# A six-stage perceiver block on one core: the first product of the closing feed-forward moved beside the last self-attention items

## The reference, cut to what matters

```python
x = x + _L1_attn_ref(_layernorm(x), L1_attn_W_Q, L1_attn_W_K, L1_attn_W_V, L1_attn_W_O)
x = x + _L1_ffn_ref(_layernorm(x), L1_ffn_k0, L1_ffn_k1, L1_ffn_k2, L1_ffn_s0, L1_ffn_s1, L1_ffn_s2)

def _L1_attn_ref(x, W_Q, W_K, W_V, W_O):      # 16 sequences of 64 rows, 16 heads of 16
    Q, K, V = x @ W_Q.T, x @ W_K.T, x @ W_V.T # then split in heads
    attn = jnp.einsum('bhqd,bhkd->bhqk', Q, K) * scale
    probs = jax.nn.softmax(jnp.where(causal, attn, -jnp.inf), axis=-1)
    return jnp.einsum('bhqk,bhkd->bhqd', probs, V) @ W_O.T   # heads joined first

def _L1_ffn_ref(x, k0, k1, k2, s0, s1, s2):   # features 1024, 1024, 256
    h = jnp.concatenate([x, -x], axis=-1)     # so k0 acts as k0[:256] - k0[256:]
    h = jax.nn.relu(s0 * _conn_dense(k0, h)) * 2
    h = jax.nn.relu(s1 * _conn_dense(k1, h)) * 2
    return s2 * _conn_dense(k2, h)            # _conn_dense: weights where(k, 1, -1)
```

## Time and profile before

| | us |
|---|---|
| median of 3 runs | 1123.73 (1123.48 to 1124.39) |
| the profiled execution's own time | 1120.75 |
| its span in the trace | 1119.0 |
| PE busy | 1037.8 (93%) |
| DVE busy | 640.2 (57%) |
| ACT busy | 472.3 (42%) |

### The profile page before, as it was taken

One profiled execution on the slowest core, in us unless ns is written; L12 is line 12 of the kernel. 1 busy time (PEld: TensorE's weight loads), 2 busy tenths in 40 slices (PEclk: granted clock), 3 DMA queues, 4 the chain that ended last, 5 costly groups with the idle time before them and its releaser, 6 DMA issues.

```text
span 1119.0 us, 27537 instructions
## 1 busy us (share of the span) xinstructions
PE 1037.8 (93%) x11715; PEld 891.8 (80%) x11715; DVE 640.2 (57%) x1376; ACT 472.3 (42%) x865; POOL 240.8 (22%) x381
## 2 busy tenths in 40 slices
PE   3899999999999899999399999997999999997998
PEld 3788888888887678887299999986878788875887
DVE  3754645545333445774669999955666643444342
ACT  1433333333333665632156776733343342344231
POOL 2212212211111124433314344433100000010000
PEclk9999999999999999996599999998999998986999
DMA  9200000000000800120227667421100002000000
GB/s 309 94 20 20 1 21 20 1 1 2 1 1 3 328 2 24 67 87 21 67 58 266 209 232 233 173 76 57 49 21 21 2 2 68 3 2 1 1 19 19
DMA packets 55672, 72.79 MB, mean 65 GB/s; under 512 B 8504, under 2 KB 48896, under 8 KB 54912
## 3 DMA queue, kind: packets, MB, share of 16 engines
q1 hardware_dynamic: 54016, 66.85, 17.7%
q0 software_dynamic: 1536, 4.20, 1.2%
HBM read 60.02 MB, written 11.01 MB: 63 GB/s over the span
## 4 chain that ended last, share of the span: by engine, by line
PE 82%; DVE 9%; ACT 4%; issue 3%; POOL 1%; DMA 1%; another core or an unknown queue 0%; SPq 0%; DVEq 0%; ACTq 0%; POOLq 0%
PE ps L603 8%; PE ps L618 8%; PE ps L2066 7%; PE ps L2082 7%; PE ps L2340 5%; PE ps L1431 4%; PE ps L587 3%; PE ps L635 3%; PE ps L1082 3%; PE ps L557 3%; PE ps L655 3%; PE ps L1349 3%; PE ps L1388 2%; PE ps L1448 2%; PE ps L1018 2%
## 5 line engine op out<-in xcount | busy, mean ns | idle before, releaser
L371 POOL TENSOR_TENSOR rn_tmp<-rn_cur,eps 128x1 f32<-128x1 f32 x48 | 13.6, 283 | 435.1 <-DVE rn_cur L365 435.0
L732 ACT ACTIVATE x0pT<-ps 128x512 f32<-128x512 f32 x64 | 38.3, 598 | 125.4 <-PE ps L618 125.4
L2066 PE MATMUL ps<-moe_xT_hi,ew_1hi 128*128 128x256 f32 x240 | 69.8, 291 | 2.3 <-DVE moe_xT_lo L2212 2.3
L2082 PE MATMUL ps<-ew_2hi,eh_hi 128*128 128x256 f32 x240 | 69.4, 289 | 2.4 <-DVE eh_lo L2220 2.4
L2218 DVE CAST eh_hi<-eh 128x512 fp32r<-128x512 f32 x60 | 61.1, 1018 | 14.1 <-ACT eh L2128 14.1
L2066 PE MATMUL ps<-moe_xT_lo,ew_1hi 128*128 128x256 f32 x240 | 68.9, 287 | 0.0
L2066 PE MATMUL ps<-moe_xT_hi,ew_1lo 128*128 128x256 f32 x240 | 68.9, 287 | 0.0
L2082 PE MATMUL ps<-ew_2hi,eh_lo 128*128 128x256 f32 x240 | 67.0, 279 | 0.0
L2082 PE MATMUL ps<-ew_2lo,eh_hi 128*128 128x256 f32 x240 | 66.9, 279 | 0.0
L830 DVE TENSOR_TENSOR x0A_lo<-ps,x0A_hi 128x512 fp32r<-128x512 f32 x64 | 41.2, 685 | 33.9 <-ACT x0A_hi L723 33.9
L2340 PE MATMUL ps<-f,ffw 128*128 128x512 f32 x256 | 59.4, 391 | 0.3 <-DVE f L2411 0.3
(11 more groups left out here) (324 smaller groups left out, 2843.0 us busy)
## 6 DMA issues: line engine op xcount, KB each, us to landing
ew<-L_ffn_W_dram SPq DMA_DIRECT2D x30, 1024.0 KB, 7.2
x0cin<-ctx_dram SPq DMA_DIRECT2D x8, 512.0 KB, 4.1
x1cin<-ctx_dram SPq DMA_DIRECT2D x8, 512.0 KB, 4.3
xg<-moe_in SPq DMA_DIRECT2D x15, 256.0 KB, 7.8
moe_out<-moe_y SPq DMA_DIRECT2D x15, 256.0 KB, 7.7
moe_in<-padneg SPq DMA_DIRECT2D x3, 1024.0 KB, 13.1
maskrow<-mask_BxS_ik_dram SPq DMA_DIRECT2D x2, 1024.0 KB, 7.6
x0wq<-L_xattn_Wq_dram SPq DMA_DIRECT2D x1, 1024.0 KB, 7.4
```

The source lines that it names most:

```text
L732: nc.scalar.activation(g.pT[:, u, :], ps[:, S_BANK[u % 2], :], ACT.Exp, scale=64.0 ** -0.5).then_inc(C0.exp, 1)
L2066: last = nc.tensor.matmul(ps[:, n % 3, j * BT:j * BT + BT], w[b % 2][:, i, f * P:f * P + P], v[b % 2][:, i, :], start=(i == 0 and m == 0), ...
L2082: last = nc.tensor.matmul(ps[:, O_BANK[b % 2] + c, 0:D], v[n % 3][:, j * BT + c * P:j * BT + c * P + P], w[b % 2][:, f, :], start=(f == 0 ...
```

## The change

The layer-0 product of the first chunk, with its relu and splits, moves from `pe_ff`, `act_ff` and `dve_ff` into iterations 21 to 24 of the loops. Its banks come from the ring, so `FILLS` gets new entries. Rows 0 to 3 are transposed in iteration 21, slices 0 to 2 are computed in iteration 22, slices 3 to 5 in 23, slices 6 and 7 in 24, and the rows of tiles 4 and 5 are transposed in 24 as well. The weights' conversions move earlier: DVE's two to iterations 18 and 19, ACT's eight pairs to iterations 18 to 21, two pairs in each. The raw bytes get another address, since the buffer `f0` at the old one is now written sooner. `FF_LAYERS` names what is left for the functions behind the loops. Their banks 2 and 3 first wait for the ring's last content there.

```diff
                 FILLS += _at(_n, "neg")
+                if _lo and _n >= _hi - 3:
+
+                    if _n == _hi - 3:
+                        FILLS += _at(_n + 2, "k", "q") + _at(_n - 1, "pv") + _ff("T", 0, 1) + _at(_n + 2, "v") + _at(_n - 1, "T", "y") + _ff("T", 2, 3)
+                    else:
+                        f = 3 * (_n - _hi + 2)
+                        FILLS += _ff("h", f, f + 1) + _at(_n - 1, "pv") + _ff("h", *range(f + 2, min(f + 3, FT))) + _ff("T", 4, 5) * (_n == _hi) + _at(_n - 1, "T", "y")
+                    continue
...
@@ pe_self
+                if span == 1 and n >= hi - 3:
+                    f = 3 * (n - hi + 2)
+                    if ahead:
+                        scores(n + 1)
+                    if n == hi - 3:
+                        fill_qk(n + 2, "k")
+                        fill_pv(n - 1, 0)
+                        fill_qk(n + 2, "q")
+                        fill_pv(n - 1, 1)
+                        ff_rows(pe, 0)
+                        ff_rows(pe, 1)
+                        fill_v(n + 2)
+                    else:
+                        ff_hidden(pe, f)
+                        fill_pv(n - 1, 0)
+                        ff_hidden(pe, f + 1)
+                        fill_pv(n - 1, 1)
+                        if f + 2 < FT:
+                            ff_hidden(pe, f + 2)
+                        else:
+                            ff_rows(pe, 4)
+                            ff_rows(pe, 5)
+                    fill_T(n - 1)
+                    if here:
+                        exponents(n)
+                    fill_y(n - 1)
+                    if n == hi - 3:
+                        ff_rows(pe, 2)
+                        ff_rows(pe, 3)
...
@@ act_self
+                if span == 1 and n > hi - 3:
+                    f = 3 * (n - hi + 2)
+                    for i in range(f, min(f + 3, FT)):
+                        ff_relu(act, i)
+                if span == 1 and n == hi:
+                    ff_upper(act, 4)
+                    ff_upper(act, 5)
                 if is_mla(n + 2):
...
                     q(n + 2)
+                    if span == 1 and n == hi - 3:
+                        ff_upper(act, 0)
+                        ff_upper(act, 1)
...
-                if span == 1 and n > lo + 1:
-                    act_ff_weights(act, n - 2 - lo)
-                if n == hi and span == 1:
-                    act_ff_weights(act, FT - 1)
+                if span == 1 and n == hi - 3:
+                    ff_upper(act, 2)
+                    ff_upper(act, 3)
+                if span == 1 and lo + 2 <= n < lo + 6:
+                    for i in range(2):
+                        act_ff_weights(act, 2 * (n - lo - 2) + i)
...
@@ dve_self
                 ahead, front, back = lo <= n + 1 < hi, n + 2 < hi, lo <= n - 1 < hi
+                if span == 1 and n == hi - 3:
+                    ff_norm(dve, 0)
+                    ff_norm(dve, 1)
                 if ahead:
                     maximum(n + 1)
+                if span == 1 and n > hi - 3:
+                    ff_split(dve, 3 * (n - hi + 2))
                 if is_mla(n + 2):
                     rotate(n + 2)
...
+                if span == 1 and n == hi - 3:
+                    for i in range(2):
+                        ff_lower(dve, i)
+                        ff_norm(dve, 2 + i)
+                if span == 1 and n > hi - 3:
+                    f = 3 * (n - hi + 2)
+                    for i in range(f + 1, min(f + 3, FT)):
+                        ff_split(dve, i)
+                if span == 1 and n == hi:
+                    ff_lower(dve, 4)
+                    ff_lower(dve, 5)
                 if routed(span, n - 4) or routed(span, n - 3):
                     route_slot_top(dve, n - 4 if routed(span, n - 4) else None, n - 3 if routed(span, n - 3) else None)
...
-                if span == 1 and n in (lo + 4, lo + 6):
-                    dve_ff_weights(dve, (n - lo - 4) // 2)
+                if span == 1 and n == hi - 3:
+                    ff_lower(dve, 2)
+                    ff_lower(dve, 3)
+                if span == 1 and n == hi - 1:
+                    ff_norm(dve, 4)
+                    ff_norm(dve, 5)
+                if span == 1 and n in (lo + 2, lo + 3):
+                    dve_ff_weights(dve, n - lo - 2)
 
...
@@ feed-forward, steps of its own
+        def ff_rows(pe, t):
+            pe.wait_ge(rn_done, ROW_BASE["mlp"] + t + 1)
+            if t < 6:
+                RS.wait_free(pe, ("ff", t), "T")
+            else:
+                RS.wait_emptied(pe, *FILLS[last_fill[t % 2]])
+            for k in range(KD):
+                last = nc.tensor.transpose(ff_bank(t)[:, k * P:k * P + P], fn[t % 2][:, k * P:k * P + P], ident)
+            last.then_inc(SA.fill if t < 6 else FF.xT_ps, 1)
+
...
+        def ff_hidden(pe, f):
+
+            if f == 0:
+                pe.wait_ge(FF.w0, KD)
+                for t in range(4):
+                    RS.wait_emptied(pe, ("ff", t), "T")
+            RS.wait_free(pe, ("ff", f), "h")
+            for k in range(KD):
+                for part in range(2):
+                    last = nc.tensor.matmul(RS.bank(("ff", f), "h"), ffw0[:, k, f * P:f * P + P], fxT[part][:, k, :],
+                                            start=(k == 0 and part == 0), stop=(k == KD - 1 and part == 1))
+            last.then_inc(SA.fill, 1)
+
+        def ff_relu(act, f):
+            if f == 0:
+                act.wait_ge(FF.scale, 2)
+            RS.wait_filled(act, ("ff", f), "h")
+            act.wait_ge(FF.h_free, f + 1)
+            nc.scalar.activation(fh[f % 2][:, :], RS.bank(("ff", f), "h"), ACT.Relu, scale=ffs[:, 0:1]).then_inc(SA.by_act, 1)
+            if f % 2 == 1:
+                RS.wait_emptied(act, ("ff", f), "h")
+                nc.scalar.activation(f0[0][:, f, :], fh[1][:, :], ACT.Copy).then_inc(FF.hi_odd, 1)
+
+        def ff_split(dve, f):
+            if f % 2 == 0:
+                RS.wait_emptied(dve, ("ff", f), "h")
+                nc.vector.tensor_copy(f0[0][:, f, :], fh[0][:, :]).then_inc(FF.hi, 1)
+            ff_split_lower(dve, f, f0, f)
+
+        def ff_split_lower(dve, n, dst, f):
+
+            if f % 2 == 0:
+                dve.wait_ge(FF.hi, n // 2 + 1)
+            else:
+                dve.wait_ge(FF.hi_odd, n // 2 + 1)
+            nc.vector.tensor_tensor(dst[1][:, f, :], fh[f % 2][:, :], dst[0][:, f, :].bitcast(F32), ALU.subtract).then_inc(FF.split, 1)
+            dve.wait_ge(FF.split, n + 1)
+            dve.sem_inc(FF.h_free, 1)
+
+        FF_LAYERS = ((0, 1), (1, 0), (1, 1))
...
```

More of the change, by code:

```diff
@@ L508, in build @@
         _more = [(n, "v") for n, (k, _) in enumerate(ITEMS) if k == "mla"] + [(n, k) for n, k in FILLS if k[0] == "A"]
+        _more += [(("ff", t), "T") for t in range(6)]
         _more += [(("x1", t), k) for t in range(T) for k in ("cT0", "q", "k1")]
@@ L512, in build @@
         QS = ps[:, 4:8, :]
+        last_fill = [max(n for n in range(len(FILLS)) if n % 4 == i) for i in range(4)]
         def bank_of(t, k):
@@ new lines, in ff_split_lower @@
+        def ff_split_lower(dve, n, dst, f):
+            if f % 2 == 0:
+                dve.wait_ge(FF.hi, n // 2 + 1)
+            else:
+                dve.wait_ge(FF.hi_odd, n // 2 + 1)
[3 more added lines that the diff above has]
+        FF_LAYERS = ((0, 1), (1, 0), (1, 1))
+        def pe_ff(pe):
+            pe.wait_ge(FF.w, 2 * FT)
+            for c, layer in FF_LAYERS:
+                if c == 1 and layer == 0:
+                    for t in range(4, 6):
+                        RS.wait_emptied(pe, ("ff", t), "T")
+                    pe.wait_ge(FF.xT, 2)
+                w, src, ks = ((ffw0, fxT, KD), (ffw1, f0, FT))[layer]
+                for f in range(FT):
+                    n = 16 * c + 8 * layer + f
+                    if c == 0 and f == 4:
+                        ff_rows(pe, 6)
+                        ff_rows(pe, 7)
+                    if n < FT + 2:
+                        RS.wait_emptied(pe, *FILLS[last_fill[2 + f]])
+                    elif n > FT + 3:
+                        pe.wait_ge(FF.r_free, n - FT - 3)
+                    for k in range(ks):
+                        if layer == 1 and f == 0:
+                            pe.wait_ge(FF.split, 16 * c + k + 1)
+                        for part in range(2):
+                            last = nc.tensor.matmul(ps[:, 2 + f % 4, :], w[:, k, f * P:f * P + P], src[part][:, k, :],
+                                                    start=(k == 0 and part == 0), stop=(k == ks - 1 and part == 1))
+                    last.then_inc(FF.r_ps, 1)
+                if layer == 0:
+                    continue
@@ new lines, in act_ff @@
+            for c, layer in FF_LAYERS:
+                dst = (f0, f1)[layer]
+                for f in range(FT):
+                    n = 16 * c + 8 * layer + f
+                    if c == 0 and f == 4:
+                        ff_upper(act, 6)
```

(22 more changed lines are left out.)

116 lines of the change are left out of this document (29 added, 87 removed).

## The result

The changed kernel takes 1103.8 us (median of 4 runs, 1102.72 to 1105.64), the kernel before in the same rounds 1123.61 (1122.82 to 1124.39): a ratio of 0.982 [0.981, 0.984], 19.8 us less.

What follows compares the result with a forecast made beforehand. PE was taken to bound the kernel. Iterations of 10.62, 9.54, 7.68 and 6.55 us start layer 1 17.5 earlier; less 0.3, 17.2 off 1120.75 gives 1103.55, and with 2.98 added 1106.5 us, range 1105.0 to 1111.0.

Steps and rivals of the forecast that it cites:

- Iteration 21: First of four iterations summed: 9.67 us of PE work, 0.88 for four added row tiles, 0.07 for maxima; 10.62 us.
- The third slice: In iteration 22, it stands where PE waited 0.82 us for DVE's division and hides that wait.
- ACT's window in iteration 23: Relu 5, copy 5 and the attention rows' copy, 1.70 us, must fit 1.95 before the output product; slack 0.25.
- The wait for row tile 3's lower part: Iteration 22's first slice waits for DVE's lower part of row tile 3: 0.2 us; a bracket over 0.3 would count against.
- The conversions: Weight conversions moved to iterations 18 to 21 were put at nothing; if their cover failed, at most 6.6 us.
- rival (c): ACT and DVE become the bound of iterations 22 to 24, up to 1 us lost in each: 1107.5 to 1109.5; 13%.
- (a): Clock dips only at the seam in iteration 24, so layer 1 starts at 1.2 GHz: 1.9 us lost, 1108.4; 12%.
- (b): Clock falls as before, near the end of iteration 22: 4 to 12 us lost, 1110.5 to 1118.5; 7%.
- (d): Slower than before: half clock from iteration 22's end that layer 1 does not lift, up to 1147 us; 2%.
- the joints between slices and narrow matmuls: Changes between wide slices and narrow matmuls in the new iterations: 0.3 us taken off the gain in all.
- the stretch: From the scores of iteration 21 to layer 1's first matmul: four iterations summed to 34.39 us, before 0.3 for joints.
- this distance: Median of the runs lies 2.98 us above the profiled execution, kept for the new kernel with an uncertainty of 1.

Runs made afterwards that it cites:

- all three slices ahead: Changed kernel with all three slices of iterations 22 and 23 (both of 24) ahead of the probabilities' product: 1110.27 us, ratio 0.989 to the kernel before.
- pairs: Changed kernel with the first two slices of iterations 22 to 24 together ahead of both halves of the probabilities' product: 1102.04 us, ratio 0.982 to the kernel before.

## Why the prediction was right and where it was wrong

**What held.** Iteration 21 took 991.50 - 980.94 = 10.56 us (10.62 forecast). The third slice hid the division. ACT's window in iteration 23 was 1.89 (1007.06 to 1008.95, 1.95 forecast); its copy ended at 1008.87, so a slack of 0.08 was left, not 0.25, and it was just enough. The wait for row tile 3's lower part was 0.33 (0.2 forecast, and just above the 0.3 named as a sign). The conversions cost nothing: iterations 18 to 20 keep 9.96 us each. The clock was 1.00 from 980 to 1040. So rival (c) did not come, nor (a) or (d). Nor did (b). The Trainium skill's "TensorE: Matmul & The Clock Gate", section "A second HAM failure mode: psum-queue depth-cycling", has the clock swing by micro-idles between groups that cycle through banks. The prediction took this to mean that the interleaved slices would fail to hold it. They cycle through the banks in three iterations, the trace shows 1.00 throughout, and PE has only three brackets in them (0.33, 0.23 and 0.47): cycling alone did not do it, and frequent idles, of which the section speaks, were not there to try it. Something like (b) did come with all three slices ahead: there the waits of 0.82 returned and the clock fell, an iteration later than (b) has it.

**The term that was mis-sized.** "I take off 0.3 for the joints between slices and narrow matmuls, which no row shows." The slices took 3.26 us in iteration 22 (1.10, 1.13, 1.03), 3.27 in 23 and 2.33 in 24, where the sum had 2.73, 2.73 and 1.82: 1.58 for joints. A further 0.12 went to the narrow halves (2.08 against 2.04, three times) and 0.13 to row tile 3; the output product gave way 0.18 earlier ahead of a slice or of layer 1 (1008.95 to 1009.73 and 1015.94 to 1016.72 are 0.78, not 0.96), twice. Iterations 22, 23 and 24 took 10.21, 8.02 and 6.99 instead of 9.54, 7.68 and 6.55, the stretch 35.78 instead of 34.69 with the 0.3. This error alone would have made the forecast too low by 1.1.

**The step that failed.** "The median of the runs shown is 2.98 above that execution, and I keep this distance." The distance was not a constant between profile and median. In the one execution that I read, the clock fell some 20.2 us behind the scores of iteration 21; in the two further traces of the kernel before, and in that with the conversions alone, it fell one iteration earlier, after some 14, and the stretch was 55.39, 55.39 and 55.38 instead of 51.95. These 3.4 us lie inside the very stretch that the change rewrites, so it removes them with the rest. With them the sum closes: 55.39 - 35.78 = 19.6 us, and 0.3 behind layer 1, against 19.8, 20.9 and 20.2 in the medians of three rounds. Kept as a distance, 2.98 was added to a kernel that no longer had it: its profiled execution was 1104.84 and its median 1103.8, and in the two further rounds its profiled execution was 0.99 below and 0.48 above the median. The two errors have opposite signs, 4.0 in the distance (2.98 forecast, -1.04 found) and 1.3 in the execution (1103.55 against 1104.84: the 1.1 of the stretch and a start of iteration 21 that came 0.65 later, less 0.4 behind layer 1), and leave the 2.7. That the miss stayed this small is luck.

I gave the distance an uncertainty of 1. The ground for more was in view: the half clock in the earlier trace rows began at the second of two like waits (0.82 in iteration 22, 1.01 in 23), and nothing in the trace said that it must be the second.

**What stays open.** Why the clock falls at the wait of iteration 22 in some executions and an iteration later in another isn't shown; four traces of the old tail give 3 to 1. How often each comes in unprofiled executions can be estimated from the mean clock in each run's record. Take (1 - clock) x span: it is 56.8 us in the mean of 63 runs of the kernel before, 40.8 in 16 of the kernel after, a difference of 16 with an error of about 1. The traces have in the clock of 980 to 1040 us 17 for the long form and 12 for the short, and 0 for the kernel after. So most executions, some four in five by this estimate, have the long form. That iteration 21 starts anywhere between 976.30 and 982.72, whatever the kernel, comes in good part from the two dips near 370 and 930, each worth 2.3 to 3.0 us; why a dip comes in one execution and not in another isn't shown either.

## What to carry to other kernels

Where a stretch runs partly at half clock, one profiled execution gives one of its lengths; look at where the fall could have come earlier or later, and put that difference in the gain and the range, since a change that cures the stretch removes it in all its forms. Dense work moved from a thin stage into another can pay twice, in the waits it covers and in the stage that it empties; here idle work in the same places paid for itself and no more. Put the filler where the wait is, not merely near it: pairs with the third slice between the product and the attention rows were 20.8 us below the kernel before, all three ahead 13.6, each against the kernel before in its own rounds.
